# Two small-head attentions: value products of 512 columns once per step, in place of 256 columns twice

## The reference

```python
q = q * cos + _rotate_half(q) * sin
k = k * cos + _rotate_half(k) * sin
scores = jnp.einsum('bhqd,bhkd->bhqk', q, k) * scale
attn = jax.nn.softmax(scores, axis=-1)
out = jnp.einsum('bhqk,bhkd->bhqd', attn, v)
```

## Time and profile before

| | |
|---|---|
| median of 3 runs | 2122.91 us |
| profiled execution | 2122.35 us, its span 2120.5 us |
| first small-head attention, steps | 105.5 to 692 us |
| causal small-head attention, steps | 1593 to 1976 us |
| TensorE busy | 1841.4 us, 87% of the span |
| VectorE busy | 1541.7 us, 73% |
| ScalarE busy | 1385.6 us, 65% |
| granted TensorE clock, mean | 0.925 of 2.4 GHz |

### The profile page before, as it was taken

One profiled execution on the slowest core, in us unless ns is written; L12 is line 12 of the kernel. 1 busy time (PEld: TensorE's weight loads), 2 busy tenths in 40 slices (PEclk: granted clock), 3 DMA queues, 4 the chain that ended last, 5 costly groups with the idle time before them and its releaser, 6 DMA issues. The chain is left out here.

```text
span 2120.5 us, 40743 instructions
## 1 busy us (share of the span) xinstructions
PE 1841.4 (87%) x16064; PEld 916.9 (43%) x16064; DVE 1541.7 (73%) x2259; ACT 1385.6 (65%) x2576; POOL 354.4 (17%) x502
## 2 busy tenths in 40 slices
PE   6699999999999579759989999999678999988585
PEld 2122222222222269725666776777312333334385
DVE  6889999999993443446877777877569979774324
ACT  3499999999999333335555656565347988877231
POOL 4100000000000150432432121211320000000123
PEclk8699999999999779969999999999869999999787
DMA  5000000000000159600000000000100000000084
GB/s 164 1 3 3 5 9 3 7 7 5 10 6 5 43 190 297 210 11 1 1 1 1 1 1 1 1 1 1 51 1 2 5 4 11 5 13 11 21 283 150
DMA packets 53278, 81.97 MB, mean 39 GB/s; under 512 B 9344, under 2 KB 38016, under 8 KB 52960
## 3 DMA queue, kind: packets, MB, share of 16 engines
q1 hardware_dynamic: 47920, 70.89, 10.5%
q0 software_dynamic: 3072, 6.30, 0.9%
q10 hardware_dynamic: 2096, 2.17, 0.4%
HBM read 64.26 MB, written 12.06 MB: 36 GB/s over the span
## 5 line engine op out<-in xcount | busy, mean ns | idle before, releaser
L726 DVE TENSOR_REDUCE a_mx<-psum 128x2 f32<-128x1024 f32 (+2 forms) x832 | 907.8, 1154 | 94.8 <-PE psum L527 59.3
L655 ACT ACTIVATE a_cs<-psum 128x512 f32<-128x512 f32 (+3 forms) x1664 | 857.8, 571 | 96.1 <-PE psum L546 51.9
L571 PE MATMUL psum<-a_cs,a_V 128*16 128x256 f32 (+1 forms) x6400 | 502.9, 385 | 11.9 <-ACT a_OD L635 9.5
L527 PE MATMUL psum<-a_KS,a_QS 48*128 48x512 bf16 (+3 forms) x1664 | 325.4, 380 | 45.8 <-DVE a_mx L726 43.3
L546 PE MATMUL psum<-a_QS,a_KS 51*128 51x512 bf16 (+3 forms) x1664 | 340.7, 379 | 7.0 <-ACT a_cs L655 3.9
L1859 PE MATMUL psum<-b_VW,b_ST 128*128 128x129 f32 x2176 | 250.0, 275 | 13.1 <-DVE X L1969 13.1
L1859 PEld LDWEIGHTS psum<-b_VW,b_ST 128*128 128x128 f32 x2176 | 245.9, 192 | 14.8 <-DVE X L1969 14.8
L546 PEld LDWEIGHTS psum<-a_QS,a_KS 51*128 51x128 bf16 x1664 | 89.4, 93 | 364.7 <-ACT a_cs L655 305.8
L1840 PE MATMUL psum<-b_GT,AT 128*128 128x512 f32 (+3 forms) x640 | 241.9, 532 | 1.6 <-ACT b_ST L1895 1.6
L571 PEld LDWEIGHTS psum<-a_cs,a_V 128*16 128x16 f32 x6400 | 107.3, 94 | 259.0 <-issue 123.5
L1944 DVE TENSOR_TENSOR b_M<-b_M,b_ST 128x512 f32<-128x512 f32 (+3 forms) x288 | 174.8, 607 | 43.4 <-ACT b_ST L1895 13.1
(11 more groups left out here) (216 smaller groups left out, 1522.2 us busy)
## 6 DMA issues: line engine op xcount, KB each, us to landing
e_W<-in_l_experts SPq DMA_DIRECT2D x46, 576.0 KB, 5.0
e_W<-in_l_experts SPq DMA_DIRECT2D x22, 768.0 KB, 5.5
yg<-e_yout SPq DMA_DIRECT2D x14, 256.0 KB, 5.6
xg<-zeros SPq DMA_DIRECT2D x2, 1472.0 KB, 9.5
a_cs<-in_rope ACTq DMA_DIRECT2D x4, 512.0 KB, 8.9
a_QS<-a_mrow SPq DMA_DIRECT2D x128, 3.0 KB
a_num<-a_OD SPq DMA_DIRECT2D x128, 16.0 KB
a_cs<-in_rope SPq DMA_DIRECT2D x1, 2048.0 KB, 8.0
```

What stands on the lines that cost most here:

```text
L527: mm = pe.matmul(ps[:, 2 * slot + half, 0:width], QS[rows, 2 * p + i, q_cols(qb, qt * P, P)], KS[rows, 2 * p + i, c * BLK:c * BLK + width] ...
L571: mm = pe.matmul(ps[32 * j:32 * j + 2 * HD, AV_BANK, a:b], V[:, kt, HPP * p + j, :], probs(e, a, b), start=(kt == 0 and half == 0), stop=last,
L655: act.activation(probs(HPP * s + j, c, BLK), ps[:, plan.bank(entry), c:BLK], ACT.Exp, scale=scale).then_inc(exp_done, 1)
L726: dve.tensor_reduce(mx[:, pk % 2, qt, 2 * i:2 * i + 2, c], banks, AX.X, ALU.max).then_inc(max_done, 1)
```

## The change

`product` loses its half argument. It issues four matmuls of all columns from the tile's first column to 512, in place of four of up to 256 columns for each half, and it is called once per step, behind the second score pair and its maxima. The waits that stood at half 0 stand at the one call. `V`, the probabilities and the PSUM bank are the same, and so are the counts of all semaphores.

```diff
--- before.py
+++ after.py
@@ -245,7 +245,6 @@
     scale = float(HD) ** -0.5
     plan = Plan(causal, order, beyond)
     NS, NPK, NOP = len(plan.steps), len(plan.packs), len(plan.operands)
-    H2 = BLK // 2
     TR = HPP * TERMS
 
     def q_cols(qb, a, n):
@@ -552,27 +551,22 @@
                         mask([plan.bank(("exp", e0 + half)) for half in range(2)], slice(c, c + P), core.neg2t,
                              s_ready, True)
 
-                def product(s, half):
+                def product(s):
 
                     pk, kt = plan.steps[s]
                     qb, p = plan.packs[pk]
-                    a, b = max(plan.first_col(s), H2 * half), H2 * (half + 1)
-                    if half == 0:
-                        if s == 0:
-                            pe.wait_ge(bank_zeroed, 1)
-                        if kt == 0 and pk:
-                            pe.wait_ge(od_done, pk)
-                        pe.wait_ge(exp_done, HPP * (s + 1))
-                    if a >= b:
-                        return
+                    a = plan.first_col(s)
+                    if s == 0:
+                        pe.wait_ge(bank_zeroed, 1)
+                    if kt == 0 and pk:
+                        pe.wait_ge(od_done, pk)
+                    pe.wait_ge(exp_done, HPP * (s + 1))
                     last = kt == plan.key_tiles(qb) - 1
                     for j in range(HPP):
                         e = HPP * s + j
-                        mm = pe.matmul(ps[32 * j:32 * j + 2 * HD, AV_BANK, a:b], V[:, kt, HPP * p + j, :],
-                                       probs(e, a, b), start=(kt == 0 and half == 0), stop=last,
-                                       skip_group_check=True)
-                    if half == 1:
-                        mm.then_inc(av_done, 1)
+                        mm = pe.matmul(ps[32 * j:32 * j + 2 * HD, AV_BANK, a:BLK], V[:, kt, HPP * p + j, :],
+                                       probs(e, a, BLK), start=(kt == 0), stop=last, skip_group_check=True)
+                    mm.then_inc(av_done, 1)
 
                 for s in range(2):
                     for j in range(2):
@@ -602,10 +596,9 @@
                         score(s, half)
                         for item in plan.halves[2 * s + half]:
                             max_item(item)
-                        if s >= 1:
-                            product(s - 1, half)
-                for half in range(2):
-                    product(NS - 1, half)
+                    if s >= 1:
+                        product(s - 1)
+                product(NS - 1)
 
             @block.scalar
             def _(act):
```

## The result

| | before | changed |
|---|---|---|
| time, median of 4 runs | 2122.50 us (2120.17 to 2125.84) | 2270.18 us (2267.32 to 2279.1) |
| ratio to before, 95% interval | | 1.0699 [1.0681, 1.0717] |
| profiled execution, time / span | 2122.35 / 2120.5 us | 2269.56 / 2267.7 us |
| mean granted clock | 0.925 | 0.902 |
| VectorE, ScalarE, TensorE busy in the first attention with maxima | 97, 95, 96% | 89, 80, 89% |

What follows compares the result with a forecast made beforehand. VectorE was taken to bound the first attention before, and a TensorE, ScalarE, TensorE chain through one PSUM bank after. 2122.35 + 79 (first attention) + 36 (causal) = 2237 us, 5.4% slower, range 2207 to 2262.

Steps and rivals of the forecast that it cites:

- What bounds before, and the new loop: Steps with maxima: VectorE's 2.28 us bounds before; afterwards a TensorE, ScalarE, TensorE chain through one bank takes 2.58 us.
- turn steps: Steps where row maxima are turned, once per pack: 3.63 us before, 3.30 after.
- The stretch with maxima: First attention up to the last turn's row copy: +73 us, of which +70 for 14 packs between first and last turn.
- the ten steps before the first turn: Start of the first attention: +3 us, 0.3 for each step.
- The 0.14 us saved per step: TensorE's product: one 512-column call costs 0.98 us against 1.12 for two of 256, saving 0.14 per step.
- The 21 steps behind the last turn: First attention's end, without maxima: steps go from 2.12 to 2.36 us, +5, plus 1 for a lower clock.
- Rival (c): TensorE's standing still lowers the clock; a tenth of some 370 steps at 1.2 GHz adds about 55: 2290 us; chance 0.05.
- The causal attention: Second attention: full steps go from 2.21 to 2.58 us, edge steps +0.23 each; +36 us together.
- (a): Faster: the fourth score does not wait, or waits in time that was free; 2091 us; chance 0.05.
- (b): Loop closes at VectorE's 2.28 us; only turns, narrow places and half the causal part lose; about 2150 us; chance 0.07.
- (d): Whole kernel: no change because both effects cancel, 2123 us; chance 0.02.

Runs made afterwards that it cites:

- the repeated run: The changed kernel once more, unaltered, on another chip with the kernel before at 2121.54: 2275.58 us, ratio 1.0726.
- a shorter exponential: Changed kernel with head 0's exponential covering 256 of 512 columns, the other half left uncomputed: 2243.7 us, ratio 1.0374 to the kernel before.
- the product inside the pair: Changed kernel with the 512-column call between the third and fourth score of a step: 2256.66 us, ratio 1.0443 to the kernel before.
- seven banks: Changed kernel with scores behind the last turn going round seven PSUM banks in place of three: 2270.62 us, ratio 1.0508 to the kernel before at 2160.6.
- the order alone: Kernel before with its two 256-column product calls both moved behind the second score pair: 2256.33 us, ratio 1.0606.
- both other places of the product: Two runs of the changed kernel, its 512-column call between the score pairs (2283.8 us) or between third and fourth score (2256.66 us).
- the new tail in the kernel before: Kernel before with one 512-column call behind both score pairs only behind the last turn of each attention: 2196.47 us, ratio 1.0161.
- The old order: Changed kernel with two 256-column calls at their old places behind the last turn of both attentions: 2234.87 us, ratio 1.0529 to the kernel before.
- the filled wait: Changed kernel with 9 pairs of unread 512-column matmuls ahead of the first attention's last turn: 2245.7 us, ratio 1.0583 to the kernel before.

## Why the prediction was wrong in size

- **What bounds before, and the new loop: right.** 1.07 to the fourth score, 0.98 for the product, 2.59 per step, 42.25 per pack, turn steps 3.2. The stretch with maxima came out at +72.1 against +73. Inside that +72.1 one term is off: the ten steps before the first turn added 1.3, not 3 (and 6 in the repeated run). Three runs moved the loop where its parts said: 2.38 with a shorter exponential, 2.37 with the product inside the pair, 1.96 with seven banks.
- **The 0.14 us saved per step: wrong in kind, without effect.** The 0.98 is right for the wide call, but it is also what two adjacent calls take (0.99). The saving comes from standing together, not from the width. Of the Trainium skill's rule on larger matmuls (Perfetto Trace Analysis, Optimizing Tensor Performance), nothing is seen at this size: 0.98 against 0.99 us.
- **The failed step: "The 21 steps behind the last turn ... will take 1.07 + 0.31 + 0.98 = 2.36."** The loop is right (2.38 at full clock), the clock was not. I added 1 us for it; it cost 25. I read 0.77 and then 1.00 in the earlier trace rows as a short dip at the turn that heals by itself, and did not ask what the new loop does if it starts at half clock. It takes 3.67 us, of which TensorE waits about 0.26 for ScalarE, and in the first attention it stayed at half clock for 76 to 81 us in every trace in which the whole product stood at one place per step and three banks met an unfilled last turn: the changed kernel twice, the order alone, both other places of the product, the shorter exponential, the new tail in the kernel before. The old order, the filled wait and the seven banks each brought the clock to 0.96 or more. The same term is missing in the causal attention (below), and the two together are most of the 33 us.
- **Rival (c) had the cause and the wrong place.** It priced half clock for a tenth of all steps, spread out: 2290. The main part, with 0.63 us of standing still per step, kept 0.99. All that was lost lay behind last turns. (Its step of 4.1 to 4.3 us was for one with maxima, of which the tail has none; the repeated run shows it, 4.10.) The case had a chance of 0.05, and the objection with which I put it there, that the steps at 665 to 692 contain waits and kept 1.00, spoke of the other order. The Trainium skill's page on this (TensorE: Matmul & The Clock Gate, A second HAM failure mode: psum-queue depth-cycling) tells of a clock that oscillates; the traces here show a steady 0.50 to 0.51 over 80 us in this tail.
- **The causal attention: +50 against +36.** Most of its packs hold (differences of the row copies in both traces): +3.2 to the first turn (forecast 3), +13.6 for the packs of 16 (13.4), +12.6 for those of 12 (12), +2.5 for those of 4 (2). Two places are off. One pack of 8 took 25.1 us against 20.35, at a clock of 0.76 against 0.92; the other three add 1.6 each on average (forecast 1.5). By its rows this is the clock too, but no run isolates it, and in the repeated run the same pack took 21.7 and its neighbour 24.1. And behind the last turn 34.6 us against 26.0, at 0.52 against 0.83, where I had put nothing. This is the tail's loss once more: the new tail in the kernel before gives the same 34.6, the old order in the changed kernel 28.4, and seven banks 20.9, at 0.87.
- **Rivals (a), (b) and (d): out.** The fourth score waits in each step, and the main part's slack covers none of it.

Left open: what sets whether a loop gets the clock back. Where it came back in the first attention (the kernel before, the old order, the seven banks, the steps with maxima at the start), TensorE's rows show no wait at half clock ahead of it. But the tail with the shorter exponential shows none either (3.46 us per step), and stayed at 0.51 for 76 us; and with the product inside the second pair the first attention's tail stayed at 0.50, the causal one's got back to 0.94 over 24.8 us, waits and all. The traces tell which loops did and which did not, not the rule.

## What to carry to other kernels

- Before merging calls, look at what lay between the users of one PSUM bank. The order of the engine's queue is also the cover for the banks' turnaround (here 1.07 us from one score to the next in the same bank), and a merged block opens a gap at whichever place it leaves; merged calls gained nothing over adjacent ones.
- A loop that follows a long wait has two prices, one at each clock level. Work out both, and do not count on its getting back to the high one; here it stayed at the low one for 80 us. Filling the wait is cheap (18 unread matmuls won 23 us here), but a later wait can undo it, as in the causal attention.
- Before speeding up the end of a stage, look at what is queued behind it: a causal attention whose last copy ended 10 us earlier moved the last output DMA by 3.

## What the runs showed of the hardware that was not expected

- One list of instructions ran at a granted clock of 0.50 for 81 us and at 1.00 for 50 us. What differed was a wait of 2.02 us ahead of it, and whether TensorE had work in it. Another list of instructions went back to 1.00 within 6 us behind a wait of 2.55 us.
- The fixed part of a product call (0.13 us, four column groups of 16 columns, fp32) is paid once per run of calls, not once per call: 0.56 for one of 256 columns, 0.99 for two, 0.98 for one of 512.
- SyncE issued the small output DMAs one per 0.67 us, and 32 of them set the end of a stage.
- The kernel before took 39 us more on two of the four chips. It was not traced there, but the other kernels' traces on these chips have 923 to 927 us between the attentions, against 886 to 891 elsewhere. Between the first gate activations of the expert stage, where ScalarE stands still for some 2 us elsewhere, it stood still for 9.4 and 13.5 us in one of them and for 8.5 and 14.2 in another. What it waited for the traces do not name.
